# A 96-step gated recurrence: batch halves laid on the two partition halves, and two matmuls of unread result in every step

## The reference, cut to what matters

```
def step(carry, xs):
    h, c = carry
    xi_t, xf_t, xg_t, xo_t = xs
    i_t = jax.nn.sigmoid(xi_t + h @ V_i)
    f_t = jax.nn.sigmoid(xf_t + h @ V_f)
    g_t = jnp.tanh(xg_t + h @ V_c)
    o_t = jax.nn.sigmoid(xo_t + h @ V_o)
    c_new = h * c + i_t * g_t
    h_new = o_t * jnp.tanh(c_new)
    return ((h_new, c_new), h_new)
(_, _), hs = lax.scan(step, (h0, c0), (xi, xf, xg, xo))
```

## Time and profile before

| | us |
|---|---|
| median of 3 runs | 1029.01 (1028.67 to 1029.68) |
| the profiled execution, its own time | 1030.23 |
| its span in the trace | 1028.5 |
| recurrence, first to last recurrent matmul (L1431) | 821.0 to 1022.4 |
| mean granted TensorE clock over the span | 0.828 of full speed |

### The profile page before, as it was taken

How to read it: one execution, slowest core, us unless ns; L and a number is a source line. 1 busy time by engine, 2 the same in 40 slices (tenths; PEclk the granted TensorE clock), 3 DMA queues, 4 the chain that set the end, 5 groups by cost and what they waited for, 6 DMA issues and landing times.

```text
span 1028.5 us, 17729 instructions
## 1 busy us (share of the span) xinstructions
PE 870.4 (85%) x5775; PEld 527.7 (51%) x5775; DVE 668.5 (65%) x1453; ACT 564.0 (55%) x1304; POOL 289.1 (28%) x233
## 2 busy tenths in 40 slices
PE   3698677447999999999289999999997788888886
PEld 3586566344232222222166565656564466666665
DVE  5836665686766767667567777777776455545543
ACT  2226666233566556556257777777775244544443
POOL 8466545470002112112123333333333311011100
PEclk9998887656999999999689999999999655555555
DMA  9600000000000000000000000000000000000000
GB/s 192 111 3 1 0 0 1 0 1 1 1 1 1 1 1 1 1 1 1 0 1 1 1 0 0 0 0 0 0 2 1 0 6 10 7 8 8 9 7 11
DMA packets 23728, 9.95 MB, mean 10 GB/s; under 512 B 17207, under 2 KB 23367, under 8 KB 23687
## 3 DMA queue, kind: packets, MB, share of 16 engines
q1 hardware_dynamic: 22598, 9.13, 4.8%
q10 hardware_dynamic: 1088, 0.26, 0.1%
HBM read 7.81 MB, written 1.57 MB: 9 GB/s over the span
## 4 chain that ended last, share of the span: by engine, by line
PE 30%; DVE 25%; ACT 10%; issue 5%; POOL 2%; DVEq 1%; ACTq 0%; POOLq 0%
PE PS L1266 8%; PE PS L1258 8%; DVE am L950 5%; DVE am L940 5%; DVE Y L956 5%; ACT Y L628 5%; PE PS L1431 3%; PE PS L1273 2%; ACT UT L651 2%; DVE UT L1007 1%; DVE UT L1005 1%; PE PS L1417 1%; DVE UT L999 1%; ACT UT L647 1%; ACT UT L645 1%
## 5 line engine op out<-in xcount | busy, mean ns | idle before, releaser
L563 ACT ACTIVATE Y<-PS,b1T 128x512 f32<-128x512 f32 x192 | 121.7, 684 | 94.9 <-PE PS L1266 94.6
L902 DVE TENSOR_TENSOR XC<-PS,Y 128x512 f32<-128x512 f32 x192 | 124.8, 686 | 72.8 <-ACT Y L563 70.0
L456 POOL TENSOR_TENSOR Y<-Y,am 96x768 f32<-96x768 f32 x64 | 93.9, 1467 | 195.7 <-DVE am L945 195.7
L1266 PE MATMUL PS<-XS,W1f 64*128 64x512 f32 x384 | 109.9, 649 | 1.2 <-ACT UF L542 1.2
L1258 PE MATMUL PS<-XC,w2s 128*64 128x512 f32 x384 | 103.6, 618 | 1.2 <-DVE XC L902 1.2
L940 DVE TENSOR_REDUCE am<-Y 96x8 f32<-96x768 f32 x64 | 60.7, 949 | 52.0 <-ACT Y L628 52.0
L435 POOL TENSOR_TENSOR st<-st,mhalf 128x8 f32<-128x8 f32 x12 | 19.7, 1638 | 243.9 <-DVE st L886 243.9
L628 ACT ACTIVATE Y<-Y 96x768 f32<-96x768 f32 x64 | 54.0, 844 | 49.7 <-DVE Y L956 49.2
L956 DVE TENSOR_TENSOR Y<-PS,am 96x384 f32<-96x384 f32 x128 | 65.2, 549 | 3.8
L950 DVE TENSOR_REDUCE am<-PS 96x8 f32<-96x768 f32 x64 | 60.6, 946 | 7.1 <-PE PS L1321 7.1
L999 DVE SCALAR_TENSOR_TENSOR UT<-UT 64x64 f32<-64x64 f32 x96 | 21.2, 221 | 66.8 <-ACT UT L647 54.4
(11 more groups left out here) (224 smaller groups left out, 1867.3 us busy)
## 6 DMA issues: line engine op xcount, KB each, us to landing
BIG<-in_x SPq DMA_DIRECT2D x8, 512.0 KB, 11.9
out<-X SPq DMA_DIRECT2D x48, 32.0 KB, 2.0
W1f<-in_L_ffn_w SPq DMA_DIRECT2D x2, 512.0 KB, 6.2
H<-in_txt SPq DMA_DIRECT2D x2, 256.0 KB, 12.2
w2s<-in_L_ffn_w SPq DMA_DIRECT2D x1, 512.0 KB, 7.1
Y<-in_L_attn_Wq SPq DMA_DIRECT2D x2, 128.0 KB, 5.9
Y<-in_L_attn_Wk SPq DMA_DIRECT2D x2, 128.0 KB, 6.4
BB<-in_L_attn_Bm ACTq DMA_DIRECT2D x2, 64.0 KB, 6.3
```

Of the source, the lines that this page charges most:

```text
L456: pool.tensor_tensor(Pn, Pn, am[:, (k - 1) % 4, 3, :].unsqueeze(2).to_broadcast([T, NH, T]), ALU.mult).then_inc(S("a_pn"), 1)
L563: act.activation(Rb[:, e % 4, :], PS[:, e % 4, :], ACT.Relu, bias=b1T[:, e:e + 1]).then_inc(S("m_r"), 1)
L902: dve.tensor_tensor(Hb[:, e % 4, :], PS[:, 4 + e % 2, :], Rb[:, e % 4, :], ALU.mult).then_inc(S("m_h"), 1)
L1266: pe.matmul(PS[:, e % 4, :], W1f[r, e, :], XD[r, q * 512:(q + 1) * 512], start=True, stop=True).then_inc(S("m_z"), 1)
```

## The change

Three things change in the recurrence.

1. Layout. The batch of 64 is cut in two halves of 32 (`HN`). Half 0 of `h`, `c` and all gates stands on partitions 0 to 63, half 1 on 64 to 127. The state tiles `Tb`, `TC`, `Cb`, `HC`, `HB` become 128 partitions by 32 columns. The recurrent weights `V3` are stored on both partition halves; each gate takes two matmuls, one a half (rows and output partitions 0 to 63, then 64 to 127), of 32 columns. i and g lie beside each other in one PSUM bank (`PS[:, 2 + par]`), so that one tanh of 128 x 64 does both; o has its own bank and its own tanh of 128 x 32.
2. Input part. `gates_x` makes one gate for four steps at a time (two matmuls of 128 columns, one a half of the batch). The three gates of the next four steps are issued in three of four steps, after the recurrent part. The loop on TensorE is written out for all 96 steps. `turn_x` uses PSUM bank 0 only, follows steps 6, 7, 9 and 10, and waits for the first copy before its third part; `copy_x` follows steps 8 and 11, and the parts of `norm` follow steps 0, 1, 3 and 4. The output (`out_tp`) is now four fp32 matmuls with the identity (weights 64 x 32) instead of one transpose.
3. Two more matmuls in every step (L1459): the bf16 identity by 3 x 128 columns of itself, into PSUM bank 1, which no instruction reads. They stand after the recurrent part and the output, ahead of `turn_x` and `gates_x`.

The core of the diff:

```diff
-                act.wait_ge(S("l_vi"), t + 1)
-                act.activation(Tb[0:64, u % 2, 0:64], PS[0:64, 2 + u % 2, 0:64], ACT.Tanh).then_inc(S("l_t"), 1)
                 act.wait_ge(S("l_vg"), t + 1)
-                act.activation(Tb[0:64, u % 2, 64:128], PS[0:64, 6 + u % 2, 0:64], ACT.Tanh).then_inc(S("l_t"), 1)
+                act.activation(Tb[:, u % 2, 0:2 * HN], PS[:, 2 + par, 2 * HN * s:2 * HN * (s + 1)], ACT.Tanh).then_inc(S("l_t"), 1)
                 act.wait_ge(S("l_vo"), t + 1)
-                act.activation(Tb[64:128, u % 2, 0:64], PS[64:128, 2 + u % 2, 0:64], ACT.Tanh).then_inc(S("l_to"), 1)
+                act.activation(Tb[:, u % 2, 2 * HN:G3], PS[:, 6 + par, HN * s:HN * (s + 1)], ACT.Tanh).then_inc(S("l_to"), 1)
...
-                dve.scalar_tensor_tensor(Cb[:, 0, :], tb[0:64, 0:64], 1.0, tb[0:64, 64:128], ALU.add, ALU.mult).then_inc(S("l_a"), 1)
+                dve.scalar_tensor_tensor(Cb[:, 0, :], tb[:, 0:HN], 1.0, tb[:, HN:2 * HN], ALU.add, ALU.mult).then_inc(S("l_a"), 1)
...
+            def gates_x(k, g):
+                if g == 0:
+                    pe.wait_ge(S("x_f"), 2 * (k // 4) + 1 + k % 4 // 2)
+                    if k >= 2:
+                        pe.wait_ge(S("l_to"), 4 * (k - 1))
...
+                for h in range(2):
+                    mm = pe.matmul(dst[64 * h:64 * h + 64], U3[:, g, :], xt[:, :, h, :], start=(g != 1), stop=(k == 0), skip_group_check=True)
...
+            def gates_h(t):
+                s, par = t % 4, t // 4 % 2
+                pe.wait_ge(S("l_h"), t)
+                for g in range(3):
+                    b, o = (2 + par, (2 * s + g) * HN) if g < 2 else (6 + par, s * HN)
+                    for h in range(2):
+                        r = slice(64 * h, 64 * h + 64)
+                        mm = pe.matmul(PS[r, b, o:o + HN], V3[r, g, :], HB[r, (t - 1) % 4, :], start=False, stop=True, skip_group_check=True)
+                    if g:
+                        mm.then_inc(S(("l_vg", "l_vo")[g - 1]), 1)
+
+            def out_tp(m):
+                pe.wait_ge(S("l_h"), 2 * m + 2)
+                if m >= 2:
+                    pe.wait_ge(S("l_out"), m - 1)
+                for a in range(2):
+                    for h in range(2):
+                        r = slice(64 * h, 64 * h + 64)
+                        o = slice(64 * a + HN * h, 64 * a + HN * h + HN)
+                        mm = pe.matmul(PS[o, 4 + m % 2, 0:D], HB[r, 2 * (m % 2) + a, :], ident[r, r], start=True, stop=True)
+                mm.then_inc(S("l_tp"), 1)
...
+            for t in range(T):
+                c, u = t // (2 * CH), t % (2 * CH)
+                if t:
+                    gates_h(t)
+                if t and t % 2 == 0:
+                    out_tp(t // 2 - 1)
+                for n in range(2):
+                    pe.matmul(PS[:, 1, 0:384], identb[:, :], identb[:, :].unsqueeze(1).to_broadcast([128, 3, 128]), start=True, stop=True)
+                if u in (6, 7, 9, 10) and c + 1 < NC:
+                    turn_x(c + 1, (6, 7, 9, 10).index(u))
+                if u % 4 and t // 4 + 1 < T // 4:
+                    gates_x(t // 4 + 1, u % 4 - 1)
```

More of the change, by code:

```diff
@@ L112, in early_fusion @@
         am = sb("am", [T, 4, 4, NH])
[L113 to L116, removed]
+        U3 = sb("U3", [D + 1, 3, D])
+        V3 = sb("V3", [128, 3, D])
         sems = {}
@@ L148, in early_fusion @@
         UTf = UT[:, :, :, :].rearrange("p k h d -> p (k h d)")
[L149 to L153, removed]
+        HN = NB // 2
+        G3 = 3 * HN
+        Tb = UTf[:, 0:2 * G3].rearrange("p (a c) -> p a c", a=2)
+        TC = UTf[:, 256:256 + HN]
+        Cb = UTf[:, 320:320 + 2 * HN].rearrange("p (a c) -> p a c", a=2)
+        HC = UTf[:, 448:448 + HN]
+        HB = UTf[:, 512:512 + 4 * HN].rearrange("p (a c) -> p a c", a=4)
         Ysum = Y1[:, 0:512].rearrange("p (m d) -> p m d", d=D)
@@ L355, in _ @@
             sp.dma_start(Wus[:, :, :], Wu.rearrange("(c p) o -> p c o", p=128)).then_inc(S("ld_at"), 16)
[L356 to L361, removed]
+            for g, (u, v, b) in enumerate(((U_i, V_i, b_i), (U_c, V_c, b_c), (U_o, V_o, b_o))):
+                sp.dma_start(U3[0:D, g, :], u).then_inc(S("ld_ls"), 16)
+                sp.dma_start(U3[D:D + 1, g, :], b.rearrange("(a n) -> a n", a=1)).then_inc(S("ld_ls"), 16)
+                for h in range(2):
+                    sp.dma_start(V3[64 * h:64 * h + 64, g, :], v).then_inc(S("ld_ls"), 16)
             for t, v, n in ((gbr, gate_b, E), (gam, gamma, D), (bet, beta, D)):
@@ L412, in _ @@
             pool.wait_ge(S("ld_at"), 16 * 6)
-            pool.wait_ge(S("ld_ls"), 16 * 9)
-            for t, f in ((bqk[:, 0, :], D ** -0.5), (UIO[:, :], 0.5), (VIO[:, :], 0.25), (VG[:, :], 0.5)):
+            pool.wait_ge(S("ld_ls"), 16 * 12)
+            for t, f in ((bqk[:, 0, :], D ** -0.5), (U3[:, 0:3:2, :], 0.5), (V3[:, 0:3:2, :], 0.25), (V3[:, 1, :], 0.5)):
                 seq(pool.tensor_scalar(t, t, f, None, ALU.mult), "wsc")
@@ L1022, in steps @@
                     cell(4 * c + u // 4, u % 4, first=first and u < 4)
-                    if u in (1, 2, 5, 6) and not last:
-                        norm(c + 1, (1, 2, 5, 6).index(u))
+                    if u in (0, 1, 3, 4) and not last:
+                        norm(c + 1, (0, 1, 3, 4).index(u))
             att_residual(0)
@@ L1403, in turn_x @@
                     pe.nop().then_inc(S("x_go"), 1)
+                if k == 2:
+                    pe.wait_ge(S("x_f"), 2 * c + 1)
                 for p in (2 * k, 2 * k + 1):
-                    mm = pe.transpose(PS[0:D, p // 4, (p % 4) * 128:(p % 4 + 1) * 128], Xnrm[:, p, :], ident[:, :])
+                    mm = pe.transpose(PS[0:D, 0, (p % 4) * 128:(p % 4 + 1) * 128], Xnrm[:, p, :], ident[:, :])
                 if k % 2:
                     mm.then_inc(S("x_tp"), 1)
[L1410 to L1449, removed]
+            def gates_x(k, g):
[3 more added lines that the diff above has]
+                        pe.wait_ge(S("l_to"), 4 * (k - 1))
+                xt = XF[:, 4 * NB * k:4 * NB * (k + 1)].rearrange("p (s h b) -> p s h b", h=2, b=HN)
+                if g < 2:
+                    dst = PS[:, 2 + k % 2, 0:8 * HN].rearrange("p (s g b) -> p s g b", g=2, b=HN)[:, :, g, :]
+                else:
+                    dst = PS[:, 6 + k % 2, 0:4 * HN].rearrange("p (s b) -> p s b", b=HN)
+                for h in range(2):
+                    mm = pe.matmul(dst[64 * h:64 * h + 64], U3[:, g, :], xt[:, :, h, :], start=(g != 1), stop=(k == 0), skip_group_check=True)
+                return mm
@@ L1453, in _ @@
             pe.wait_ge(S("a_h"), 4 * NC)
[L1454 to L1460, removed]
+            gates_x(0, 0)
+            gates_x(0, 1).then_inc(S("l_vg"), 1)
+            gates_x(0, 2).then_inc(S("l_vo"), 1)
+            for t in range(T):
[10 more added lines that the diff above has]
+                    gates_x(t // 4 + 1, u % 4 - 1)
+            out_tp(NM - 1)
 _INS = ["x", "txt", "L0_tok_W", "L0_tok_b", "L0_attn_Win", "L0_attn_bin_", "L0_attn_Wout", "L0_attn_bout",
```

25 lines of the change are left out of this document (13 added, 12 removed).

## The result

The changed kernel takes 1041.57 us (median of 4 runs, 1041.37 to 1043.78) against 1028.84 us before in the same measurement: ratio 1.0128, 95% interval 1.011 to 1.0145. It is slower by 12.7 us. The forecast was 1006 and faster; the measured time lies above its range and near the 1046 of the first rival, the low clock.

A forecast was written before the change was run, and what follows sets the result against it. A ring of waits that no engine fills, 2.10 us a step, bounds the recurrence. 95 x (2.10 - 1.78) = 30.4, less 2.9, 4.1 and 0.5, takes 22.9 us off 1030.23; median 1006, range 992 to 1028.

The forecast's parts named there:

- the first rival: Recurrence: clock stays low and the unread pair is the bound, 2.2 to 2.55 us a step, 1046 us; chance 0.09.
- the ring: One recurrence step's chain of waits through TensorE, ACT and DVE, filled by no engine: 2.10 us, to become 1.78.
- The TensorE part: From h to the i-and-g tanh: eight matmul instructions waited for, 0.65 us against 0.63 before, bounds 0.53 to 0.82.
- the first term: Time from the end of h to the start of the first recurrent matmul: 0.15 us.
- the short instruction that it put at 0.20: Time for one short recurrent matmul instruction to go through TensorE before the i-and-g tanh: 0.20 us.
- The queue: TensorE's in-order work per step at the high clock: recurrent 0.55, output 0.35, unread pair 0.46, input 0.50 us.
- the 2.9 us for its overruns: Even steps with input part take 1.86 to 1.9 us of TensorE work, 0.12 over 1.78: 24 x 0.12 = 2.9 us.
- the third rival: High clock, but TensorE's work bounds the steps through input halves in sequence or real drains: 1015 to 1030 us; chance 0.08.
- Does the clock rise?: Claim that TensorE gets the high clock for nearly all of the recurrence; the forecast outcome had chance 0.66.
- the state of 805.60: Before the recurrence: 24 transposes end to end for 5.2 us at the low clock, the clock rising at their end.
- no thinner than the bursts from 813.40: Claim that 1.2 to 1.9 us of work per 1.78 holds the clock like 1.06 us transpose bursts with idle gaps.
- a change of shape cheap: Tiling changes three or four times a step on TensorE cost little; full drains of 0.2 us each would give 1028 us.

The follow-up runs named there:

- run with twelve and then three: Changed kernel with twelve unread matmuls instead of two in step 0 and three in each later step: 990.57 us, ratio 0.9626.
- run with four small weights: Changed kernel with four unread matmuls a step instead of two, with weights of 64 x 64 instead of 128 x 128: 1095.21 us in one run.
- run with four on the whole array: Changed kernel with four unread matmuls a step instead of two, weights still 128 x 128: 1001.63 us in one run.
- run with twelve and then two: Changed kernel with twelve unread matmuls instead of two in step 0, two in each later step: 1039.62 us, ratio 1.0098.
- the same kernel: Changed kernel with twelve unread matmuls in step 0, then 5, 4, 2, 4 by step, two fewer in transpose steps: 1003.15 to 1032.0 us in four executions.

## Why the prediction was wrong

**The view of the ring was right.** The forecast said that no engine filled the 2.10 us and that each part would shrink. At the high clock the parts were predicted as 0.65, 0.25, 0.43, 0.26 and 0.19, together 1.78. They measured 0.52, 0.26, 0.45, 0.26 and 0.19, together 1.68, inside the bounds of 1.66 to 1.95. One tanh fewer and the narrower DVE work came as computed (192 ns against the forecast of 183, 230 against 227 for the tanh of c). The TensorE part was priced 0.13 too high, and 0.10 of it is the first term: the forecast let 0.15 go by between h and the first matmul, as in the earlier trace rows, and it is 0.05 (960.96 to 961.01), at either clock; why was not looked into. From the first matmul to the tanh it is 0.47 (961.01 to 961.48) against 0.52. The forecast's saving of 0.08 for 64 columns twice at twice the clock should have been 0.05; the short instruction that it put at 0.20 measures 0.22.

**The queue was right at the low clock and too dear at the high one.** At the high clock the forecast had 0.55, 0.35, 0.46 for a pair and 0.50; the runs with a high clock show 0.47, 0.24, 0.43 and 0.38. That is 1.52 where the forecast had 1.86, so a queue with the pair would not overrun a ring of 1.68 outside the transposes, and the 2.9 us for its overruns would be nothing. At the low clock, worked out for the rival, it had 0.79, 0.5 with the transposed output, 0.74 and 0.5 to 1.0; the changed kernel has 0.78, 0.37, 0.75 and 0.63, and its 2.26 a step stands at the low end of the rival's 2.2 to 2.55. The input part on 65 rows, the third rival, costs less than either of the forecast's prices (0.96 without overlap, 0.50 with it): 0.38 for four instructions of 128 columns at the high clock.

**Had the clock been high, the forecast would have been too slow.** Its 1006 less 9.5 (95 x 0.10 of ring) and 2.9 (the overruns) is 993.6, an estimate. The run with twelve and then three, the nearest to it with a high clock throughout, took 990.6, below the whole range. Two sums in the forecast are also off by 2 to 3 us, with no bearing on the outcome: by its own terms a step of 1.66 gives 995 and not 992, and 9 us less than the kernel before is 1020 and not 1018.

**The step that failed is "Does the clock rise?"**, and in it one inference: that TensorE queued up without a gap at the low clock is in the state of 805.60, after which the clock rose. It isn't. The changed kernel shows 20.00 of 20 us covered at clock 0.50 in every such window from 820 to 1020. The run with four small weights shows it apart from coverage: against the run with four on the whole array it has the same number of matmuls and columns, every 20 us from 840 to 1080 covered, and no rise. What stood at 805.60 was 24 transposes with 128 x 128 weights; what fills the changed kernel is for more than half recurrent, output and input matmuls on 64 x 64, 64 x 32 and 65 x 64 weights. A row of the trace of before that I had not weighed says this already:

```profile
215.00:224.00 9.00, 8.59 (x60) 7.42 (x60) 6.65 (x9) 2.74 (x5) 8.92 (x4) 0.50 0.01 2
```

There TensorE is covered for 8.59 of 9 us, mostly by matmuls of 16 columns, and the clock stays at 0.50. Four transposes with 128 x 128 weights stand between every two groups of these. The window in the earlier trace rows, 17.66 of 20 at 0.50, was listed for the rival and then put down to the remaining gaps.

**The second half of that step failed too.** The forecast held the pair, on the high clock, to be "no thinner than the bursts from 813.40". The run with twelve and then two had the high clock given to it and lost it after four steps. So both the rise and the holding failed, and either alone would have been enough.

**The chances.** The low clock had 0.09 and is what happened. The argument for the high clock rested on two stretches of the trace and none of them had small tiles in it; 0.66 was too much for that. The sign turned because 95 x (2.10 - 1.90) of ring at the low clock, the gain which the run without the pair shows as 16 us, is less than the 28 us that the pair costs there.

**Small instructions and changes of shape.** Twelve recurrent instructions take 0.47 us at the high clock, the change of shape behind them included, 0.04 each. The Trainium skill (TensorE: Matmul & The Clock Gate, section "Wait — 56ns, not 53.3ns?") gives about 62 ns a matmul where firmware decodes the instructions; no run here shows that price.

The forecast called a change of shape cheap, since in the earlier trace rows the next row starts 0.07 before the last one ends. But a row's end includes the transit, so this start is already late. What a change costs is seen against the run with four small weights, where in odd steps none comes between the recurrent part and the unread matmuls:

```profile
901.59 0.79 PE L1431 MATMUL PS<-UT,V 64*64 64x32 f32 x10
902.19 1.46 PE L1459 MATMUL PS<-identb 64*64 64x384 bf16 x4
```

The last recurrent instruction, 0.29 long, starts 0.50 into its row, at 902.09, and the unread matmul follows 0.10 later. In the changed kernel the last one of 897.54 starts at 898.10, and the unread matmul with 128 x 128 weights follows at 898.32, 0.22 later. So a change costs some 0.12 us at the low clock, an estimate from these rows; with four of them in an even step with input part that is about 0.5 of its 2.53. The Trainium skill (TensorEngine Tiling (Array Packing), "Key Properties") says that changing the tiling mode drains the engine. The trace agrees, at less than the 0.2 a change that the forecast tried. These waits are not what kept the clock low in the run with small weights: it has fewer of them than the run with four whole-array matmuls, whose clock rose.

What stays open: how the clock's grant weighs array, columns and time was not measured, only single points of it. The run with small weights changes rows and columns together, and was not tried with the clock already high. The runs with one, three (without the twelve), four and four small, and the pair on the kernel before, are single executions, and near the edge one execution can differ from the next. And no kernel with the old layout at the high clock was tried, so how the gain of the best version (39 us) would split there isn't known; on the new layout it is 16 us from the layout at the low clock and some 23 us from the clock.

## What to carry to other kernels

Work that is added to raise TensorE's clock pays only beyond the point where the clock moves; short of it, every matmul of it is paid at the slow rate as soon as the engine's queue is the longest path (none 1013.8, one 1020.5, two 1041.6, three 1070.2, four 1001.6 us; one, three and four in single runs). So read the granted clock after such a change before anything else, try more of it as well as less, and keep a clock that is already high across the start of the stage: here less sufficed to hold it than to raise it. A row that covers TensorE's time says neither that the engine works near its rate nor that the clock will rise.

## What the runs showed of the hardware that was not expected

- Small weights don't lift the clock: four matmuls of 384 columns a step with 64 x 64 weights left it at 0.50 (1095.2 us), with 128 x 128 weights it rose to 1.00 (1001.6 us).
- Holding is easier than raising: three a step hold the high clock (990.6 us) and did not raise it in one run (1070.2 us); two did not even hold it (1039.6 us).
- Near the edge the same kernel gave 1003.15, 1012.9, 1028.31 and 1032.0 us.
- Twelve fp32 matmul instructions with 64 x 64 weights on the two diagonal quarters of the array go through in 0.47 us at the high clock and 0.78 at the low one, weight loads and the change of shape behind them included.
- A change of shape between neighbouring matmuls costs some 0.12 us at the low clock: 0.22 between two starts with it, 0.10 without it.
